# Value product of the last stage from high and low parts in fp32r, with the square kept whole in PSUM

## What is computed

```python
x = x + 0.5 * ffn(layernorm(x))
x = x + attn(layernorm(x))
x = x + 0.5 * ffn(layernorm(x))

def ffn(x):                      # x_prev: x one token back, zero ahead of the first
    xr = mu_r * x + (1 - mu_r) * x_prev
    xk = mu_k * x + (1 - mu_k) * x_prev
    r = sigmoid(xr @ W_r.T)                    # "receptance"
    k_act = square(relu(xk @ W_k.T))           # "key", squared
    return r * (k_act @ W_v.T)                 # "value"

def attn(x):                     # keys, values: 64 quaternions per token
    keys = unit(x @ Wk.T + bk); values = x @ Wv.T + bv
    memory = cumsum(quat_mul(values, keys), axis=1)
    ret = quat_mul(memory, conj(keys)) / sqrt(position)
    return x + (layernorm(ret) * g + b) @ Wo.T + bo
```

## Time and profile before

| | before |
|---|---|
| median of 3 runs | 663.1 us (663.0 to 664.0) |
| profiled execution | 662.2 us |
| its span | 660.5 us |
| mean granted TensorE clock | 0.987 |
| busy TensorE, VectorE, ScalarE, GpSimd | 628.1, 563.1, 429.3, 545.0 us |
| HBM, mean over the span | 28 GB/s |

### The profile page before, as it was taken

How to read it: one execution, slowest core, us unless ns; L and a number is a source line. 1 busy time by engine, 2 the same in 40 slices (tenths; PEclk the granted TensorE clock), 3 DMA queues, 4 the chain that set the end, 5 groups by cost and what they waited for, 6 DMA issues and landing times.

```text
span 660.5 us, 12424 instructions
## 1 busy us (share of the span) xinstructions
PE 628.1 (95%) x3456; PEld 531.5 (80%) x3456; DVE 563.1 (85%) x1170; ACT 429.3 (65%) x792; POOL 545.0 (83%) x626
## 2 busy tenths in 40 slices
PE   7899999999989999999999999999797999999997
PEld 6689989989866777777777777777576988998996
DVE  5979999998878999999999999999967787887773
ACT  3856776776565766666766666766375677677762
POOL 3498898897749999999999999999946789889863
PEclk9989999999999999999999999999897999999999
DMA  8740000000000000000000000000000111111111
GB/s 254 229 124 0 0 0 0 0 1 0 1 1 0 1 1 1 0 0 0 0 0 0 0 0 0 0 0 0 0 1 1 65 54 42 64 45 50 65 64 65
DMA packets 19257, 18.66 MB, mean 28 GB/s; under 512 B 1312, under 2 KB 19232, under 8 KB 19232
## 3 DMA queue, kind: packets, MB, share of 16 engines
q1 hardware_dynamic: 19232, 18.36, 8.6%
HBM read 9.97 MB, written 8.39 MB: 28 GB/s over the span
## 4 chain that ended last, share of the span: by engine, by line
PE 55%; POOL 5%; DVE 3%; issue 3%; ACT 3%; POOLq 0%; DVEq 0%; ACTq 0%
PE bank L1207 14%; PE bank L1118 14%; PE bank L1149 8%; PE bank L1253 7%; PE bank L1234 3%; PE bank L1227 3%; ACT m_xnT L844 2%; PE bank L1132 2%; PE bank L1209 2%; PE bank L1201 2%; POOL rhalf L283 1%; POOL bhalf L263 1%; POOL rhalf L284 1%; POOL bhalf L264 1%; PE bank L1255 1%
## 5 line engine op out<-in xcount | busy, mean ns | idle before, releaser
L1207 PE MATMUL bank<-wkv,m_xnT 128*128 128x256 f32 x512 | 132.9, 389 | 8.9 <-ACT m_xnT L844 8.5
L1207 PEld LDWEIGHTS bank<-wkv,m_xnT 128*128 128x128 f32 x512 | 90.6, 192 | 32.5 <-ACT m_xnT L844 16.2
L1149 PE MATMUL bank<-wffn,kact 128*128 128x256 f32 x512 | 116.0, 379 | 0.4 <-DVE kact L426 0.4
L1149 PEld LDWEIGHTS bank<-wffn,kact 128*128 128x128 f32 x512 | 94.9, 190 | 12.3 <-issue 0.6
L297 POOL TENSOR_TENSOR xk_lo<-xk,xk_hi 128x1024 fp32r<-128x1024 f32 x30 | 71.1, 2370 | 33.0 <-ACT xk_hi L758 33.0
L1017 POOL TENSOR_TENSOR xr_lo<-xr,xr_hi 128x1024 fp32r<-128x1024 f32 x32 | 76.1, 2378 | 13.9 <-ACT xr_hi L764 12.5
L1024 POOL TENSOR_TENSOR res<-res,gating_buffers 128x1024 f32 (+1 forms) x31 | 74.7, 2409 | 13.7 <-DVE gating_buffers L433 12.5
L599 DVE TENSOR_TENSOR xn<-bank,khat 128x1024 f32<-128x1024 f32 x64 | 77.7, 1216 | 2.2
L599 DVE TENSOR_TENSOR gating_buffers<-bank,khat 128x1024 f32<-128x1024 f32 x64 | 77.4, 1209 | 0.0
L1118 PE MATMUL bank<-wffn_hi,xr_hi 128*128 128x256 f32 x256 | 72.3, 282 | 0.0
L1118 PE MATMUL bank<-wffn_hi,xr_lo 128*128 128x256 f32 x256 | 72.1, 282 | 0.0
(11 more groups left out here) (129 smaller groups left out, 1617.8 us busy)
## 6 DMA issues: line engine op xcount, KB each, us to landing
res<-x SPq DMA_DIRECT2D x16, 512.0 KB, 4.4
out<-res SPq DMA_DIRECT2D x15, 512.0 KB, 2.9
out<-res SPq DMA_DIRECT2D x2, 256.0 KB, 2.1
wo<-w_o SPq DMA_DIRECT2D x1, 256.0 KB, 4.6
wffn<-w_k SPq DMA_DIRECT2D x1, 256.0 KB, 4.3
wffn<-w_r SPq DMA_DIRECT2D x1, 256.0 KB, 4.5
wffn<-w_v SPq DMA_DIRECT2D x1, 256.0 KB, 5.3
wkv<-w_kv SPq DMA_DIRECT2D x1, 256.0 KB, 5.6
```

The source lines that it names most:

```text
L1149: last = nc.tensor.matmul(dst[:, i, :], x[:, f, i * P:(i + 1) * P], wffn[:, w, f, :], start=f == 0, stop=f == FC - 1)
L1207: nc.tensor.matmul(dst[:, i, :], m_xnT[:, f, i * P:(i + 1) * P], wkv[:, f, col:col + D], start=f == 0, stop=False)
```

## The change

Only the last stage's value product changes, with what feeds it. Value is made of three fp32r products for each float32 one: high by high, low by high and high by low part, 24 products for a tile in place of 8. The square's high part is the old VectorE product, now written in fp32r (`kact_hi`). Behind it ScalarE writes the whole square into PSUM over k (`whole_square`, from `relu_k`), and VectorE subtracts the high part from it into `kact_lo` (`square_low`). These two low parts stand between the first and the second receptance mix in VectorE's order, and `value` waits for them. GpSimd splits the halved W_v at the set-up, ahead of its first low part, and TensorE waits for that split before the last stage's second tile.

```diff
--- before.py
+++ after.py
@@ -100,6 +100,8 @@
         wffn = sb("wffn", [P, 3, FC, D])
         wffn_hi = sb("wffn_hi", [P, 2, FC, D], F32R)
         wffn_lo = sb("wffn_lo", [P, 2, FC, D], F32R)
+        wv_hi = sb("wv_hi", [P, FC, D], F32R)
+        wv_lo = sb("wv_lo", [P, FC, D], F32R)
         cols = sb("cols", [P, 7 * FC])
         lng, lnb = (cols[:, i * FC:(i + 1) * FC] for i in (2, 3))
         cols_less_one = sb("cols_less_one", [P, 2 * FC])
@@ -174,6 +176,8 @@
         rprod = gating_buffers[:, :, :].rearrange("p i (c n) -> p i c n", n=Q)
         bhalf = sb("bhalf", [P, 2, 2, D])
         rhalf = sb("rhalf", [P, 2, 2, D])
+        kact_hi = sb("kact_hi", [P, FC, CW], F32R)
+        kact_lo = sb("kact_lo", [P, FC, CW], F32R)
         bound = kact[:, :, :].rearrange("p b (t n) -> p b t n", n=D)
         ret = sb("ret", [P, 2, 2, D])
         normed = sb("normed", [P, 2, D])
@@ -209,6 +213,9 @@
         wkv_in = sem("wkv_in")
         consts_pool = sem("consts_pool")
         setup = sem("setup")
+        value_weights_halved = sem("value_weights_halved")
+        value_high_ready = sem("value_high_ready")
+        value_low_ready = sem("value_low_ready")
         lnb_folded = sem("lnb_folded")
         bias_lines_ready = sem("bias_lines_ready")
         bias_rows_ready = sem("bias_rows_ready")
@@ -223,7 +230,7 @@
 
         FFN_SEMS = ["st_done", "stats_done", "var_done", "rstd_done", "shift_done", "xn_done", "T_done", "carry_done", "xnT_done",
                     "diff_done", "xk_done", "xkhi_done", "xklo_done", "xr_done", "xrhi_done", "xrlo_done", "k_done",
-                    "relu_done", "kact_done", "r_done", "gate_done", "v_done", "gated_done", "res_done"]
+                    "relu_done", "kact_done", "ksquare_done", "klow_done", "r_done", "gate_done", "v_done", "gated_done", "res_done"]
         ffn_sems = [{n: sem(f"f{i}_{n}") for n in FFN_SEMS} for i in range(2)]
         MEM_SEMS = ["x_st_done", "x_mv_done", "x_moments_done", "x_var_done", "x_power_done", "x_std_done", "x_rstd_done", "x_scales_done", "st_done", "mv_done", "std_done", "rstd_done", "xn_done", "T_done", "xnT_done",
                     "res_done", "K_done", "V_done", "ksq_done", "ksum_done", "above_done", "knorm_done",
@@ -351,7 +358,7 @@
 
                 dve.wait_ge(consts_in, 16 * 3)
                 nc.vector.tensor_scalar(cols_less_one[:, :], cols[:, 0:2 * FC], -1.0, None, ALU.add)
-                nc.vector.tensor_scalar(wffn[:, 2, :, :], wffn[:, 2, :, :], 0.5, None, ALU.mult)
+                nc.vector.tensor_scalar(wffn[:, 2, :, :], wffn[:, 2, :, :], 0.5, None, ALU.mult).then_inc(value_weights_halved, 1)
                 own(nc.vector.tensor_copy(wffn_hi[:, :, :, :], wffn[:, 0:2, :, :]))
 
             def split_weights_low(first, end):
@@ -418,12 +425,20 @@
                     nc.vector.scalar_tensor_tensor(dst[:, f, :], diff[:, f, :], mu_less_one[:, f:f + 1], xT_ps[:, f, :],
                                                    ALU.mult, ALU.add).then_inc(e[done], 1)
 
+                def square_low(j, b, o):
+
+                    s = 2 * j + b
+                    dve.wait_ge(e["ksquare_done"], 2 * s + o + 1)
+                    nc.vector.tensor_tensor(kact_lo[:, o, :], k_ps[:, o, :], kact_hi[:, o, :].bitcast(F32),
+                                            ALU.subtract).then_inc(e["klow_done"], 1)
+
                 def square(j, b, o):
 
                     s = 2 * j + b
                     dve.wait_ge(e["relu_done"], 2 * s + o + 1)
                     need(dve, e["v_done"], 2 * s)
-                    nc.vector.tensor_tensor(kact[:, o, :], relu_k[:, o, :], k_ps[:, o, :], ALU.mult).then_inc(e["kact_done"], 1)
+                    dst = kact if stage == 0 else kact_hi
+                    nc.vector.tensor_tensor(dst[:, o, :], relu_k[:, o, :], k_ps[:, o, :], ALU.mult).then_inc(e["kact_done"], 1)
 
                 def gating(j, b):
                     s = 2 * j + b
@@ -501,6 +516,10 @@
                             square(j, b, 1)
                         if mixing:
                             mix_receptance(nj, nb, 0)
+                        if stage == 1:
+                            square_low(j, b, 0)
+                            square_low(j, b, 1)
+                        if mixing:
                             mix_receptance(nj, nb, 1)
                         if first:
                             stats_of(1, 1)
@@ -769,6 +788,12 @@
                     need(act, e["kact_done"], 2 * s)
                     nc.scalar.activation(relu_k[:, o, :], k_ps[:, o, :], ACT.Relu).then_inc(e["relu_done"], 1)
 
+                def whole_square(j, b, o):
+
+                    s = 2 * j + b
+                    act.wait_ge(e["kact_done"], 2 * s + o + 1)
+                    nc.scalar.activation(k_ps[:, o, :], relu_k[:, o, :], ACT.Square).then_inc(e["ksquare_done"], 1)
+
                 def keep_moments(j, b):
                     s = 2 * j + b
                     act.wait_ge(m["x_mv_done"], s + 1)
@@ -791,6 +816,9 @@
                             keep_moments(j - 1, b)
                         relu(j, b, 0)
                         relu(j, b, 1)
+                        if stage == 1:
+                            whole_square(j, b, 0)
+                            whole_square(j, b, 1)
                         if first:
                             normalize(1, 0)
                         if has(b, 1):
@@ -1073,6 +1101,11 @@
             inverse_std, _, first_block, ffn_steps = ffn(0)
             inverse_std(0, 0)
             inverse_std(0, 1)
+            pool.wait_ge(value_weights_halved, 1)
+            nc.gpsimd.tensor_copy(wv_hi[:, :, :], wffn[:, 2, :, :]).then_inc(value_high_ready, 1)
+            pool.wait_ge(value_high_ready, 1)
+            nc.gpsimd.tensor_tensor(wv_lo[:, :, :], wffn[:, 2, :, :], wv_hi[:, :, :].bitcast(F32),
+                                    ALU.subtract).then_inc(value_low_ready, 1)
             first_block()
             ffn_steps()
             _, inverse_std_of_two, first_block, last_ffn_steps = ffn(1)
@@ -1163,6 +1196,16 @@
                 def value(j, b):
 
                     s = 2 * j + b
+                    if stage == 1:
+                        pe.wait_ge(e["klow_done"], 2 * s + 2)
+                        need(pe, e["gated_done"], s)
+                        for i in range(CT):
+                            last = parts(v_tok[:, i, :],
+                                         lambda f: kact_hi[:, f, i * P:(i + 1) * P], lambda f: kact_lo[:, f, i * P:(i + 1) * P],
+                                         lambda f: wv_hi[:, f, :], lambda f: wv_lo[:, f, :])
+                            if i % 2:
+                                last.then_inc(e["v_done"], 1)
+                        return
                     pe.wait_ge(e["kact_done"], 2 * s + 2)
                     need(pe, e["gated_done"], s)
                     by_token(v_tok, kact, 2, 0, CT // 2).then_inc(e["v_done"], 1)
@@ -1336,6 +1379,7 @@
                 pe.wait_ge(rprod_done[1], MS)
 
             def memory_stored():
+                pe.wait_ge(value_low_ready, 1)
                 pe.wait_ge(m["x_done"], MS)
 
             ffn_steps(last_output, memory_stored)
```

## The result

The changed kernel takes 676.7 us, the median of four runs (676.0 to 677.5), against 663.1 us: a ratio of 1.0207, 95% interval 1.0182 to 1.0231. The forecast was 676.8 us. The profiled execution took 676.0 us with a span of 674.2.

What follows compares the result with a forecast made beforehand. TensorE bounds the last stage before; after, a closed loop through value. Start -1.5, twelve periods +14.3, tile 14 +1.2, tile 15 -0.3 make +13.7 on 662.2 us profiled: 675.9, plus 0.9 for the median: 676.8; range 672 to 688.

Steps and rivals of the forecast that it cites:

- The bound: Last stage: TensorE alone is on the path; the squares end only 0.21 us before value starts.
- The products: Value in each of 16 tiles: 24 fp32r products take 2.85 us against 3.45, 0.60 less per tile.
- When value starts: Full tile: value waits for the second low part, starts at 8.32, 1.79 us later; next transposes at 11.17, +1.19 per tile.
- the -0.41 from tile 14's value to tile 15's: Stage's end: tile 14's value 0.60 us shorter, tile 15's value starting 0.19 us later.
- The whole square: ScalarE writes it into PSUM at 0.59 us each, ending before the low parts start; it costs nothing.
- the middle stage's 1.11: Rival: Square takes 1.11 us in contiguous form too, +0.5 us per tile, 684 us; chance 8%.
- rival 3: ScalarE: Square needs another activation table than Sigmoid, two loads per tile, +0.3 us per tile, 681 us; chance 3%.
- The start of the stage: Last stage's first tiles: value(1) ends at 516.0 us in place of 517.5, so -1.5 us.
- the prediction's choice between two ends: Stage's start: key(1) at full clock gives -1.5 us, at half clock +0.8; -1.5 was taken.
- Set-up: GpSimd's weight copy and subtraction, 2.8 us together, fit in its 4.58 us idle time and cost nothing.
- Rival 1: TensorE's clock falls in the new gap, losing 1.7 us each time: 688 us in half the tiles, 699 in all; chance 14%.
- Rival 5: Last stage: low parts are out when receptance ends, tiles 9.38 us apart, 9.6 less, 653.5 us; chance 4%.

Runs made afterwards that it cites:

- run 3: Changed kernel with low parts written to a tile nobody reads; value reads a constant low part and waits for the squares alone: 658.4 us.
- run 4: Changed kernel without whole squares and low parts; the 24 products read a constant low part and wait for the squares alone: 654.3 us.
- run 2: Changed kernel with both low parts ahead of both receptance mixes in VectorE's order: 671.5 us.
- run 1: Changed kernel with both low parts behind both receptance mixes in VectorE's order: 701.2 us.
- run 7: Changed kernel with value's 16 high-part products first, waiting for the squares alone, and the 8 low-part products last: 660.9 us.
- run 8: Run 7 with Sigmoid ahead of the receptance cast in ScalarE's order: 658.9 us.
- run 9: Run 8 with the next key input's cast also ahead of the whole squares in ScalarE's order: 657.2 us.
- run 5: Run 1 with four float32 products on zeros added in the gap ahead of value: 688.6 us.

## Why the prediction was right

- **The bound.** The slack of 0.21 us between square and value was the right thing to look at. Runs 3 and 4 bear it out: without the wait the work of the change is done in less time than the kernel took before.
- **The products.** 2.85 was forecast, 2.97 measured behind a wait, 2.88 without (run 4). The first product after an idle stretch takes 0.22 and not 0.12 (613.78 to 614.00).
- **When value starts.** 8.32 was forecast, 8.23 measured. The low parts' start and length were right to 0.01; the step off was the handing over from VectorE to TensorE. I took 0.14 from the stage's first tile; in a full tile it is 0.06 (613.72 to 613.78), in the first tile it is 0.14 again. This miss and the last one cancel: 11.17 was forecast, 11.20 measured. The sum was better than two of its terms, which is luck. The same holds for the -0.41 from tile 14's value to tile 15's: value got shorter by 0.48 and not 0.60, and the last value started 0.08 later and not 0.19.
- **The whole square.** 0.60 us per ACTIVATE into PSUM (1.20 for two), against 0.59 taken from the Relu; the middle stage's 1.11 did not apply. The estimate by the Trainium skill, page "ScalarE: Activation LUTs", section "What ACT_TABLE_LOAD costs", was 0.61, and the trace agrees (0.602 on average). In the whole run there are three table loads as before, so rival 3 was empty.
- **The start of the stage.** -1.5 was forecast, -1.37 measured. Value(0) took 4.43 us, partly at the lower clock, and the clock was back when key(1) began:

```profile
500.12 0.36 PE L1151 MATMUL bank<-wv_hi,kact_hi 128*128 128x256 f32 x1 [3.56 <-DVE kact_lo L432]
504.55 1.04 PE L1165 MATMUL bank<-ident,xn 128*128 128x128 f32 x8
506.63 0.50 PE L1151 MATMUL bank<-xk_hi,wffn_hi 128*128 128x512 f32 x1 [1.05 <-POOL xk_lo L304]
```

  Key(1) takes 2.90 us to receptance (509.53), against 5.29 before. So the clock did fall right behind the gap ahead of value(0), and it was back for key(1), as the prediction's choice between two ends had it. The other end exists: in run 2 value(0) came after 2.90 us idle and ran in 2.94 us at full clock, key(1) took 4.19, partly at the lower clock, and value(1) ended 36.70 us after the stage's first transposes, not 35.84.
- **Set-up.** GpSimd's cast took 0.61 us and its subtraction 1.28, and its low part behind them still had 2.33 us of idle ahead. It costs nothing, as forecast.
- **Rival 1, the clock,** did not come in the changed kernel, but run 1 shows how near it was: with the low parts one mix of 0.66 us further back, it takes 15 us. A chance of 14% was no exaggeration. The lower level lasted some 3.4 us each time, as the prediction had it, but a fall cost value 1.2 to 1.5 us, not 1.7.
- **Rival 5** (TensorE stays the bound) needed what runs 7 to 9 then gave it, other orders. The prediction held the idle of VectorE useless for this since it lies ahead of the square's chain; in runs 7 to 9 it is used all the same, because value no longer waits for the end of that chain.

## What to carry to other kernels

Before swapping a costly instruction for cheaper ones that need one more step of preparation, look at the slack between the operand's last producer and its consumer: here 0.21 us, against 1.8 us of new steps, and a gain of 0.57 per tile became a loss of 1.2. Then issue first the part of the work that does not need the new operand: 16 of 24 products cover the wait. And read an engine in a tight loop by what stands in its queue ahead of an instruction whose input is ready: moving two ScalarE instructions past others gave the last 3 to 4 us.

## What the hardware showed

TensorE's clock can fall in short, regular idle stretches. With 1.54 us idle in each tile of 11.20 it stayed at 2.4 GHz for 118 us; with 2.10 to 2.24 us in tiles otherwise 11.86 long (run 1) it fell to 1.2 GHz in ten of thirteen tiles, and each fall cost 1.2 to 1.5 us more in the product behind the gap. The Trainium skill, page "TensorE: Matmul & The Clock Gate", section "A second HAM failure mode: psum-queue depth-cycling", speaks of such swings with short idles between groups; run 1 agrees (0.90 over 120 us), the changed kernel itself does not show it (1.00). The length of the gap alone does not decide: tiles 2 and 7 of run 1 idled 2.24 and 2.23 us without a fall, tile 12 idled 2.10 and had one. Nothing between 1.58 and 2.10 us, repeated in every tile, was tried. Four dummy products in the gap (run 5) brought 12.6 us back.
